# Row maxima of the second eight attention heads beside the exponentials of the first eight, with their shuffled rows sent through memory

## What is computed

```python
Q = (X @ Wq.T + bq).reshape(B, S, H, d_head) * scale
K = (X @ Wk.T + bk).reshape(B, S, H, d_head) * scale
V = (X @ Wv.T + bv).reshape(B, S, H, d_head)
scores = jnp.einsum('bqhd,bkhd->bhqk', Q, K)
causal = jnp.tril(jnp.ones((S, S), bool))
scores = jnp.where(causal[None, None], scores, -jnp.inf)
attn = jax.nn.softmax(scores.astype(jnp.float32), axis=-1).astype(X.dtype)
out = jnp.einsum('bhqk,bkhd->bqhd', attn, V).reshape(B, S, D)
return out @ Wo.T + bo
```

## Time and profile before

| | us |
|---|---|
| median of 3 runs | 1651.46 |
| lowest and highest | 1650.98, 1653.03 |
| profiled execution, its own time | 1658.11 |
| its span, first to last instruction | 1656.3 |
| TensorE busy in the span | 1406.0 (85%) |
| VectorE busy | 1159.5 (70%) |
| ScalarE busy | 827.7 (50%) |
| GpSimd busy | 784.9 (47%) |

### The profile page before, as it was taken

How to read it: one execution, slowest core, us unless ns; L and a number is a source line. 1 busy time by engine, 2 the same in 40 slices (tenths; PEclk the granted TensorE clock), 3 DMA queues, 4 the chain that set the end, 5 groups by cost and what they waited for, 6 DMA issues and landing times. The chain is left out here.

```text
span 1656.3 us, 38451 instructions
## 1 busy us (share of the span) xinstructions
PE 1406.0 (85%) x14366; PEld 1000.5 (60%) x14366; DVE 1159.5 (70%) x2384; ACT 827.7 (50%) x2173; POOL 784.9 (47%) x1112
## 2 busy tenths in 40 slices
PE   5987995596555989999999999999999999976575
PEld 2443344464423657677777777777777777764464
DVE  5888117573566787888888888888888888833623
ACT  2333982224033655666665665666666666632122
POOL 5101001487024366457567566566566656633443
PEclk9998998699776999999999999999999999977787
DMA  8200005282724454564654664655556556331883
GB/s 278 85 2 2 1 1 155 89 249 107 251 51 98 109 146 114 149 158 127 161 158 129 150 154 140 146 155 148 141 152 156 130 151 171 89 91 58 247 253 130
DMA packets 249433, 218.72 MB, mean 132 GB/s; under 512 B 88770, under 2 KB 224962, under 8 KB 247200
## 3 DMA queue, kind: packets, MB, share of 16 engines
q1 hardware_dynamic: 234992, 192.41, 43.1%
q0 software_dynamic: 5712, 15.60, 2.8%
q10 hardware_dynamic: 8544, 8.26, 1.6%
HBM read 133.85 MB, written 82.25 MB: 130 GB/s over the span
## 5 line engine op out<-in xcount | busy, mean ns | idle before, releaser
L1974 DVE SCALAR_TENSOR_TENSOR d_conv<-d_big,all_cw,d_conv 128x1023 f32<-128x1023 f32 (+2 forms) x192 | 245.3, 1278 | 46.2 <-ACT d_conv L2216 44.3
L1696 PE MATMUL d_big<-all_xn_t,all_w 128*128 128x512 f32 x512 | 251.8, 622 | 18.6 <-DVE d_conv L1974 11.8
L1696 PEld LDWEIGHTS d_big<-all_xn_t,all_w 128*128 128x128 f32 x512 | 93.7, 198 | 102.3 <-issue 89.0
L2450 POOL TENSOR_TENSOR d_y<-d_y,all_xn 128x256 f32<-128x256 f32 x128 | 97.8, 764 | 110.2 <-DVE d_y L2126 92.1
L2315 ACT COPY d_ys<-d_big 128x128 f32<-128x128 f32 x256 | 60.9, 266 | 178.3 <-PE d_big L1864 140.7
L1902 PE MATMUL d_big<-all_wo,d_yt 128*128 128x256 f32 x512 | 125.9, 391 | 13.8 <-DVE d_yt L2051 13.8
L1835 PE MATMUL d_big<-all_w,all_xn_t 128*128 128x256 f32 x512 | 124.3, 387 | 0.0
L2407 POOL TENSOR_TENSOR d_vs<-d_vs,d_sv 128x1024 f32<-128x1024 f32 x32 | 61.3, 1915 | 131.3 <-DMA d_vs<-turned_v_scratch 130.0
L1902 PEld LDWEIGHTS d_big<-all_wo,d_yt 128*128 128x128 f32 x512 | 97.1, 197 | 26.5 <-issue 14.3
L1835 PEld LDWEIGHTS d_big<-all_w,all_xn_t 128*128 128x128 f32 x512 | 94.5, 192 | 19.8 <-issue 8.8
L2025 DVE SCALAR_TENSOR_TENSOR d_AI<-d_big,d_b_col,d_decay 128x256 f32<-128x256 f32 x256 | 104.3, 474 | 1.4 <-PE d_big L1709 0.6
(11 more groups left out here) (451 smaller groups left out, 3552.8 us busy)
## 6 DMA issues: line engine op xcount, KB each, us to landing
turned_kq_scratch<-d_turned SPq DMA_DIRECT2D x32, 512.0 KB, 3.8
d_kq_tok<-turned_kq_scratch SPq DMA_DIRECT2D x128, 128.0 KB, 3.0
turned_v_scratch<-d_vs SPq DMA_DIRECT2D x16, 1024.0 KB, 4.1
d_vs<-turned_v_scratch SPq DMA_DIRECT2D x64, 256.0 KB, 5.6
grouped_y_scratch<-d_yx SPq DMA_DIRECT2D x32, 512.0 KB, 3.4
d_yx<-grouped_y_scratch SPq DMA_DIRECT2D x128, 128.0 KB, 3.2
all_w<-in_L_attn_W_qkvz SPq DMA_DIRECT2D x16, 768.0 KB
l_hold<-in_L_ffn_gate_up_proj SPq DMA_DIRECT2D x48, 192.0 KB, 3.3
```

The source lines that it names most:

```text
L1696: mm = pe.matmul(big[0][:, c, :], w_sb[par][:, k, n * DK:(n + 1) * DK], xn_t[:, k, c * 512:(c + 1) * 512], start=(k == 0), stop=(k == KD - 1))
L1974: dve.scalar_tensor_tensor(conv[:, sh:T], src[:, 0:T - sh], cw[:, bass.ds(g, 1), COLUMN_OF[j], 3 - sh], conv[:, sh:T], ALU.mult, ALU.add). ...
L2450: pool.tensor_tensor(part, part, zs[:, t, :], ALU.mult).then_inc(s["yg_s"], 1)
```

## The change

The two blocks become one. The first part does heads 0 to 7 as before. The maxima of heads 8 to 15 are found in 96 pieces of at most 512 columns (one bank each, three banks in turn), of which 12 come before the first exponentials and 84 are spread over the first 20 of the 24 steps of heads 0 to 7. Tiles of more than 512 keys have two pieces, whose maxima one VectorE instruction joins (`join_pieces`). In these 24 steps the exponentials' scores have three banks, afterwards six again. The rows of heads 8 to 15 are not turned by TensorE and cast by ScalarE: the two units with their parts are written to memory (two DMAs of 768 KB), and 14 DMAs of 256 KB, one for each of the seven slots of queries and of keys, bring them back in the shape of `q_rows` and `k_rows`, each to 16 partitions, in runs of 2 KB. They stand in SyncE's queue ahead of the sends of the maxima. The second maxima are transposed after step 20 and wanted by the scores of head 8, issued in step 23. GpSimd's layout of the values comes in the same block, the additions of the output bias move to the third quad, and VectorE's copy and division are placed apart. The core of the diff (the parts moved without a change are left out):

```diff
@@ -154,55 +154,106 @@
+        neg_part = m.sb("neg_part", [P, 2, HALF, TT // 2])
...
+        o_t = rest[0][:, :].rearrange("p (c n) -> p c n", c=2)
...
+        part_dram = nc.dram_tensor("query_key_scratch", [2, P, 3, T], BF16, kind="Internal").ap()
...
-        for h in range(H0):
-            side += [("turn", h + 1, quarter) for quarter in range(4 if h + 1 < H0 else 0)]
-            side += [("values", h)] if h < TT else []
-            side += [("maxima", 0)] if h == HALF else []
+        for h in range(HALF):
+            side += [("turn", h + 1, quarter) for quarter in range(4 if h + 1 < HALF else 0)]
+            side += [("values", h)]
...
+        pieces = [(h, q, c) for h in range(HALF, H0) for q in range(TT) for c in range(q // 4 + 1)]
+        NP = len(pieces)
+        FIRST, SPREAD = 12, 20
...
+        MIXED = 2 * PER
...
+        def width_of(q, c):
+
+            return min(512, (q + 1) * P - 512 * c)
+
+        def probs_bank(n):
+
+            return bank[3 + n % 3] if n < MIXED or n % 6 < 3 else bank[n % 3]
+
+        def share(at):
+
+            done = [min(NP, FIRST + (NP - FIRST) * (at + k) // SPREAD) for k in range(2)]
+            return range(done[0], done[1])
+
+        block = ctx.enter_context(nc.Block())
...
             clear_slots(sp)
-            send_maxima(sp, 0)
+            for n in range(2):
+                sp.wait_ge(split_s, 3 * (2 + n) + 3)
+                sp.dma_start(part_dram[n], part[2 + n][:, :, :]).then_inc(part_out[n], 16)
+            sp.wait_ge(ones_set, 4)
+            for n in range(2):
+                sp.wait_ge(part_out[n], 16)
+                for r, slot in enumerate(SLOTS):
+                    sp.dma_start((q_rows, k_rows)[n][r * DH:(r + 1) * DH, HALF:H0, :],
+                                 part_dram[n].rearrange("(h d) j t -> d h j t", d=DH)[:, :, slot[n], :]).then_inc(rows_in, 16)
+            send_maxima(0)
+            send_maxima(1)
+            sp.wait_ge(max_in[1], 48)
 
         @block.gpsimd
...
+            pool.wait_ge(v_out, TT)
+            for g in range(QUADS):
+                if g >= 2:
+                    pool.wait_ge(pv_done, (g - 1) * PER)
+                for j in range(4):
+                    pool.tensor_copy(v_quad[:, g % 2, :, j, :], v_aug[:, :, g * 4 + j, :]).then_inc(vq_set, 1)
...
+            def piece(k):
+                h, q, c = pieces[k]
+                if k == 0:
+                    pe.wait_ge(rows_in, 16 * 2 * len(SLOTS))
+                if k < 2:
+                    side_free(len(side) - 2 + k)
+                elif k == 2:
+                    pe.wait_ge(s_max, HROW - 1)
+                else:
+                    pe.wait_ge(piece_max, k - 2)
+                n, diag = width_of(q, c), c == q // 4
+                mm = pe.matmul(bank[k % 3][:, 0:n], q_rows[0:MAXROW, h, q * P:(q + 1) * P],
+                               k_rows[0:MAXROW, h, c * 512:c * 512 + n], start=True, stop=not diag, skip_group_check=True)
+                if diag:
+                    mm = pe.matmul(bank[k % 3][:, n - P:n], ident_bf[:, :], neg_upper[:, :], start=False, stop=True,
+                                   skip_group_check=True)
+                mm.then_inc(piece_mm, 1)
...
-            def scores(g, i):
+            def score(g, i, j):
-                if i == 0 and g % 2 == 0:
+                n = g * PER + 4 * i + j
+                if i == 0 and j == 0 and g % 2 == 0:
                     pe.wait_ge(max_in[g // 2], 48)
-                for j in range(4):
-                    n = g * PER + 4 * i + j
-                    buf = bank[n % NST]
-                    if n >= NST:
-                        pe.wait_ge(exp_done, n - NST + 1)
-                    off = q0 - c * 512
-                    diag = q0 == k * P
-                    mm = pe.matmul(buf[:, off:512], k_rows[0:MAXROW + 3, g * 4 + j, k * P:(k + 1) * P],
-                                   q_rows[0:MAXROW + 3, g * 4 + j, q0:(c + 1) * 512], start=True, stop=not diag,
+                if n < 3:
+                    pe.wait_ge(s_max, HROW)
+                elif n < MIXED + 3:
+                    pe.wait_ge(exp_done, n - 2)
+                elif n < MIXED + 6:
+                    pe.wait_ge(piece_max, NP)
+                    pe.wait_ge(maxp, 8)
+                else:
+                    pe.wait_ge(exp_done, n - 5)
+                off = q0 - c * 512
+                diag = q0 == k * P
+                mm = pe.matmul(probs_bank(n)[:, off:512], k_rows[0:MAXROW + 3, g * 4 + j, k * P:(k + 1) * P],
+                               q_rows[0:MAXROW + 3, g * 4 + j, q0:(c + 1) * 512], start=True, stop=not diag,
+                               skip_group_check=True)
+                if diag:
+                    mm = pe.matmul(probs_bank(n)[:, off:off + P], ident_bf[:, :], neg_lower[:, :], start=False, stop=True,
                                    skip_group_check=True)
-                    if diag:
-                        mm = pe.matmul(buf[:, off:off + P], ident_bf[:, :], neg_lower[:, :], start=False, stop=True,
-                                       skip_group_check=True)
-                    mm.then_inc(st_mm, 1)
+                mm.then_inc(st_mm, 1)
 
...
+            for quarter in range(4):
+                turn_rows(0, quarter)
+            for h in range(HALF):
+                for q in range(TT):
+                    rows_scores(h, q)
+                    if h + 1 < HALF and 1 <= q <= 4:
+                        turn_rows(h + 1, q - 1)
+                    if h + 1 == HALF and q == 2:
+                        values_of(h)
+                if h + 1 < HALF:
+                    values_of(h)
+            for k in range(3):
+                piece(k)
+            turn_maxima(0)
+            for k in range(3, FIRST):
+                piece(k)
+            for j in range(4):
+                score(0, 0, j)
             for at, (g, i) in enumerate(order):
-                if at + 1 < len(order):
-                    scores(*order[at + 1])
+                mine = share(at)
+                for j in range(4):
+                    if at + 1 < len(order):
+                        score(*order[at + 1], j)
+                    if j < len(mine) - 1:
+                        piece(mine[j])
                 values(g, i)
+                if len(mine):
+                    piece(mine[-1])
+                if at == SPREAD:
+                    turn_maxima(1)
                 if i == first_k[1] + 1:
...
@@ -511,6 +493,22 @@
...
+            for h in range(HALF):
...
-                        act.activation(probs[:, n % NPB, off:512], bank[n % NST][:, off:512], ACT.Exp).then_inc(exp_done, 1)
+                        act.activation(probs[:, n % NPB, off:512], probs_bank(n)[:, off:512], ACT.Exp).then_inc(exp_done, 1)
...
+            def piece(k):
+                h, q, c = pieces[k]
+                dve.wait_ge(piece_mm, k + 1)
+                found = neg_max[:, h, q:q + 1] if q < 4 else neg_part[:, c, h - HALF, q - 4:q - 3]
+                dve.tensor_reduce(found, bank[k % 3][:, 0:width_of(q, c)], AX.X, ALU.max, negate=True).then_inc(piece_max, 1)
+
+            def join_pieces():
+                dve.wait_ge(piece_max, NP)
+                dve.tensor_tensor(neg_max[:, HALF:H0, 4:TT], neg_part[:, 0, :, :], neg_part[:, 1, :, :], ALU.min).then_inc(joined, 1)
...
+            def keep(g, c):
+                dve.wait_ge(pv_done, g * PER + 4 * last_k[c] + 4)
+                if g:
+                    dve.wait_ge(o_turned, g * 2 + c - 1)
+                dve.tensor_copy(o_t[:, c, :], bank[6]).then_inc(o_copied, 1)
+
+            def divide(g, c):
+                dve.wait_ge(o_turned, g * 2 + c + 1)
+                if g:
...
+            for u in range(2 * KD):
+                split(u)
+            for h in range(HALF):
+                for q in range(TT):
+                    maxima(h, q)
+                    if q == 0 and h:
+                        values_of(h - 1)
+                    if q == 4 and h + 1 == HALF:
+                        values_of(h)
+            for k in range(3):
+                piece(k)
+            split_maxima(0)
+            for k in range(3, FIRST):
+                piece(k)
+            for at, (g, i) in enumerate(order):
+                for k in share(at):
+                    piece(k)
+                if at + 1 == SPREAD:
+                    join_pieces()
+                if at == SPREAD:
+                    split_maxima(1)
+                if g == 2 and i < TT:
+                    dve.tensor_tensor(x[:, i, :], x[:, i, :], o_bias[:, :], ALU.add).then_inc(b_added, 1)
                 for c in range(2):
-                    dve.wait_ge(pv_done, g * PER + 4 * last_k[c] + 4)
-                    if g:
-                        dve.wait_ge(o_turned, g * 2 + c - 1)
-                    dve.tensor_copy(o_t[:, c, :], bank[6]).then_inc(o_copied, 1)
-                    dve.wait_ge(o_turned, g * 2 + c + 1)
```

(15 more changed lines are left out.)

314 lines of the change are left out of this document (138 added, 176 removed).

## The result

Against the kernel before on the same chip the changed kernel took 1635.99 us (median of 20 runs, 1623.06 to 1648.43) to 1652.76 (20 runs, 1646.96 to 1678.93): ratio 0.988, 95% interval 0.9859 to 0.9901, thus about 20 us faster (16 to 23). (The ratio is formed from the fast runs, 19 of the 20 of the changed kernel, and is not quite that of the two medians.) On the 1651.46 us of the prediction that is 1631.6: faster, inside the range, 7.6 us above the forecast. The profiled execution has a span of 1634.5 us. Had only the time been looked at, it lies nearer to the coupling rival (1636) than to the forecast (1624.0); the stages decide otherwise.

What follows compares the result with a forecast made beforehand. VectorE was taken to bound the maxima, TensorE and ScalarE almost together the exponentials. Terms -53.3 + 3.5 + 17.2 + 1.5 + 1.0 + 2.4 = -27.7, taken as -27.5 from 1651.46, gave 1624.0 us; range 1618.5 to 1635.5.

Steps and rivals of the forecast that it cites:

- coupling rival: Mixed stage: engines exchanging three banks each way lose a wide reduction in each of 20 steps, +12 us, 1636; chance 0.17.
- First stage, -53.3: Row maxima: the first stage loses heads 8 to 15 and ends at 102.1 instead of 155.36, -53.3 us.
- Last maximum to first score, 5.9: Between maxima and exponentials: twelve pieces, split and sends take 5.9 us instead of 2.45, +3.5 us.
- The mixed steps, 44.05 + 17.2 + 1.5 + 1.0 and the stall 2.4: Exponentials of heads 0 to 7: present 44.05 us, plus pieces 17.2, three banks 1.5, slow clock 1.0, stall 2.4.
- Clock +1.0: Start of the mixed stage: TensorE begins at the lower clock, where pieces cost double, +1.0 us.
- Stall +2.4: Before head 8: sending the second maxima takes 5.3 us, two narrow steps cover 2.9, leaving a stall of +2.4 us.
- Rows through memory, 0: Row transfers for heads 8 to 15: loads land at 76, wanted at 102, so they cost 0.
- Nothing from the rest: Moved value copies, bias additions and the missing barrier cost nothing extra; the second half of exponentials keeps its 43.6 us.
- Wrong: ... a later stage that changes its length: Listed sign, no size given: a later stage changing its length would show the prediction wrong.
- Better than the sum: Mixed stage: ScalarE's backlog covers the stall and narrow steps even out, 4 us less, 1620; chance 0.12.
- Clock: Rival, mixed stage: short bank waits keep TensorE at 1.2 GHz, up to +59 us, 1683 at worst; chance 0.04.
- rows late: Rival, row loads: served one after another they end at 112 (1634) or 195 (1717, slower); chance 0.04.

Runs made afterwards that it cites:

- x_dve: Changed kernel, VectorE reducing only 64 columns of each of the 84 mixed-stage pieces, TensorE computing them in full: 1640.05 us, mixed stage 63.3 us.
- x_both: Changed kernel, the 84 mixed-stage pieces cut to 64 columns for both TensorE and VectorE: 1619.23 us, mixed stage 54.5 us.
- b42s17: Changed kernel with pieces spread over 17 steps instead of 20, four banks for scores and two for pieces: 1639.76 us, ratio 0.9913 to the kernel before.
- inter: Changed kernel with one value matmul behind each score in mixed steps that do not start a sum of values: 1675.04 us, ratio 1.0081 to the kernel before.
- b42i: Changed kernel with the order of inter, and four banks for scores and two for pieces: 1675.97 us, ratio 1.0112 to the kernel before.
- r_place: Changed kernel with four scratch tensors of the second attention declared first: 1626.45 us, one run.
- b_rows: Kernel before, only the rows of heads 8 to 15 sent through memory instead of turned: 1648.39 us, ratio 0.9965.
- r_before: Kernel before, unchanged, run and profiled again: 1657.12 us to 1655.97, ratio 0.9995.
- r_after: Changed kernel, unedited, run and profiled again: 1632.72 us, ratio 0.986 to the kernel before.
- s17: Changed kernel with its pieces spread over 17 steps instead of 20: 1633.94 us, ratio 0.9844 to the kernel before.
- x_pe: Changed kernel, TensorE computing only 64 unmasked columns of each of the 84 mixed-stage pieces, VectorE reading full width: 1624.54 us, mixed stage 56.7 us.

## Why the prediction was right, point by point

It was right in direction, in its range and in the main in its mechanism; the time came 7.6 us above the forecast. In the profiled execution 2.5 of that are the attention's: +2.1 in the first stage, -1.2 in the mixed one, +1.6 behind the stall. The first and the last of these come and go with the execution (points 1 and 5). The rest of the 7.6 lies outside the part that I summed.

1. *First stage, -53.3.* From first to last maximum 55.1 us (forecast 53.0), before 106.3: -51.2. In head 0 the granted clock was 0.67 (46 to 50 us) and VectorE waited 0.77 and 1.20 us where it had waited 0.21. That is of the execution: in six of the ten profiles with this stage unchanged (x_dve, x_both, b42s17, inter, b42i, r_place) it lasted 53.4 us, in the other four 54.5 to 55.7. b_rows shows 5.5 us a head in place of 5.4.
2. *Last maximum to first score, 5.9.* 101.48 to 107.36 us: 5.9.
3. *The mixed steps, 44.05 + 17.2 + 1.5 + 1.0 and the stall 2.4: 66.2 from first score to head 8's.* 107.36 to 172.35: 65.0. The terms hold as a sum with TensorE full. Taken singly they do not: three banks alone cost 8.6 (7.9 against r_before), and the pieces on top of them 10.2. My sentence that the banks bite only in steps 20 to 23 is true only because pieces fill the other steps' gaps. The gaps of TensorE that I let cancel against VectorE's local waits are seen: 15.0 us of waits of its weight loads for reductions (much of it beside a matmul still running), and only 3.9 us (65.0 - 61.09) in which no matmul runs, the stall among them.
4. *Clock +1.0.* 0.50, 0.90, then 1.00 from 112, as told. What it cost was not measured apart.
5. *Stall +2.4.* 3.15 us on ScalarE, against about 0.6 without: 2.5. What I left out is what can follow a stall: the clock at 0.71 and 0.86 behind it, and a second half of 45.2 us in place of 43.6. By the marks of the table that is 44.7 in place of 43.2. The half is 43.2 in every other profile, those with the stall among them. In r_after a stall of 3.22 us (TensorE busy 1.44 of 4) was followed by a granted clock of 1.00. So this execution alone paid the 1.6. I had also taken the stall for a loss that a better spread would win back; in s17 it is gone, and the denser steps before it take as much more.
6. *Rows through memory, 0.* Landed by 85, not 76, wanted at 101; the cost in the attention is 0, as b_rows shows. The estimate by the Trainium skill's "SBUF — State Buffer", section "Door 1: The DMA port swizzle", was 90 at 104 GB/s; 130 GB/s were moved, so the trace is between the two. What the step missed is its side effect: the tensor that it declares moves others, and one wait in the second attention grew by 1.3 to 2.4.
7. *Nothing from the rest.* This is the step that failed. "Wrong: ... a later stage that changes its length" was on my list, and it did: the rest's median is 6.1 us longer (1416.9 to 1410.8). Less the longer wait, some 4 us (an estimate) stay open.

*Rivals.* Coupling (+12) did not come: the mixed stage is shorter than the forecast. Its mechanism is real, though; b42s17, with one bank less for the pieces, pays 6.3 us for it. *Better than the sum* did not come: r_after against r_before gains 27.7 us, which is the sum itself, and the shortest attention with this order, that of r_place, 28.8, where the rival had 4 us more than the sum. *Clock* and *rows late* did not come.

## What to carry to other kernels

When work of a free engine is laid over a stage, sum the engine that works in both, and check the answer by the stage and not by the time: here the time pointed to one rival while the stage excluded it. Costs that fill each other's gaps (banks too few, extra matmuls) must be summed from a full engine, and taking one away alone gives back less than it seems to cost; so it went with the stall, with x_pe and with the banks. And a scratch tensor is not free of side effects: it moves its neighbours, and a wait elsewhere can change with them.

## What was not expected of the hardware

Four value matmuls that write 32 columns each took 1.07 us together and one took 1.04 (inter): apart, each costs what four cost together. A load of 256 KB was 1.3 to 2.4 us longer under way, until its reader started, when another tensor had been declared before its source (9.4 to 9.5 us in three profiles, 10.8 to 11.8 in ten), and with the order of declaration alone changed it was back at 9.5 (r_place, one profile). Fourteen loads into 16 partitions each, all in flight, moved 130 GB/s.
